# Experts' weights summed by group in one matmul per batch and spread over the partitions by loads from DRAM

## The reference

```python
x = x + tanh(g_xattn[1]) * xattn1(layernorm(x), ctx, mask)
x = x + tanh(g_ffn[1]) * moe(layernorm(x), ...)
# moe, for each token:
probs = softmax(x @ gate_weight.T)                 # 32 experts
top_val, top_idx = top_k(probs, 8); top_val /= sum(top_val)
w_tg = sum over the chosen of top_val, by merge_groups[top_idx]    # 8 groups
gate, up = split(x @ gate_up_proj[dominant_experts].T)   # 8 groups of 192 rows each
act = silu(gate) * up
out = sum over groups g of w_tg[:, g] * (act[:, g] @ down_proj[dominant_experts][g].T)
```

## Time and profile before

| | us |
|---|---|
| median of 3 runs | 1887.24 (1886.98 to 1889.6) |
| profiled execution | 1887.19 |
| span of the profiled execution | 1885.4 |
| TensorE busy in the span | 1846.4 (98%) |
| VectorE busy | 995.9 (53%) |
| ScalarE busy | 538.6 (29%) |
| GpSimd busy | 323.5 (17%) |

### The profile page before, as it was taken

The page is one execution under the profiler, slowest core; times in us unless marked ns, Lnnn a source line. Parts: engine busy times, 40 slices in busy tenths (PEclk is TensorE's granted clock), DMA queues, the critical chain, the costliest instruction groups (busy, mean ns, idle before and its releaser), DMA issues.

```text
span 1885.4 us, 24612 instructions
## 1 busy us (share of the span) xinstructions
PE 1846.4 (98%) x9552; PEld 905.6 (48%) x9552; DVE 995.9 (53%) x2036; ACT 538.6 (29%) x801; POOL 323.5 (17%) x299
## 2 busy tenths in 40 slices
PE   8799999999999999999999999999999999999999
PEld 3445554644444444444444444444444444444444
DVE  5676776754554455454436554545445455554422
ACT  3224433312221122122112233233333223333321
POOL 1123322222021120202010011111111111111111
PEclk9899999999999999999999999999999999999999
DMA  5124433333414223340310200101010101000000
GB/s 159 55 62 129 140 118 95 96 129 65 104 42 127 90 68 104 70 125 27 90 54 9 76 1 23 32 1 54 1 54 1 54 1 54 1 23 1 1 23 23
DMA packets 135830, 112.10 MB, mean 59 GB/s; under 512 B 75554, under 2 KB 92066, under 8 KB 135714
## 3 DMA queue, kind: packets, MB, share of 16 engines
q1 hardware_dynamic: 135714, 110.53, 19.7%
HBM read 78.00 MB, written 32.51 MB: 59 GB/s over the span
## 4 chain that ended last, share of the span: by engine, by line
PE 83%; issue 9%; DVE 3%; POOL 2%; DMA 2%; ACT 1%; POOLq 0%; SPq 0%; DVEq 0%; ACTq 0%
PE bank L923 44%; PE bank L1012 17%; PE bank L1092 10%; PE bank L992 4%; PE bank L932 3%; PE bank L977 1%; POOL arena L897 1%; PE bank L958 1%; PE bank L1079 1%; PE bank L1027 1%; POOL arena L871 0%; PE bank L1054 0%; DVE arena L1278 0%; DMA arena<-in_L_xattn_Wkv 0%; DMA arena<-x_after_ffn 0%
## 5 line engine op out<-in xcount | busy, mean ns | idle before, releaser
L923 PE MATMUL bank<-arena 128*128 128x512 f16 x4608 | 1042.2, 380 | 8.4 <-DVE arena L1299 7.3
L923 PEld LDWEIGHTS bank<-arena 128*128 128x128 f16 x4608 | 451.1, 98 | 538.9 <-DVE arena L1299 7.8
L1012 PE MATMUL bank<-arena 128*128 128x512 f16 x1536 | 352.1, 379 | 1.2 <-DVE arena L1506 1.2
L1092 PE MATMUL bank<-arena 128*128 128x512 f16 x1152 | 264.3, 379 | 0.9 <-POOL arena L897 0.9
L1648 DVE SCALAR_TENSOR_TENSOR arena<-bank,arena 128x512 f32<-128x512 f32 x96 | 72.0, 750 | 329.0 <-PE bank L923 329.0
L1191 ACT ACTIVATE arena<-bank,arena 128x512 f32<-128x512 f32 x128 | 99.5, 778 | 493.5 <-PE bank L923 490.5
L1012 PEld LDWEIGHTS bank<-arena 128*128 128x128 f16 x1536 | 150.1, 98 | 181.1 <-DVE arena L1506 1.7
L897 POOL TENSOR_TENSOR arena<-arena 128x512 f16<-128x512 f32 x96 | 111.0, 1157 | 626.0 <-ACT arena L1228 626.0
L1504 DVE TENSOR_SCALAR arena<-arena 128x512 f16<-128x512 f32 x128 | 65.8, 514 | 281.6 <-ACT arena L1191 281.3
L1092 PEld LDWEIGHTS bank<-arena 128*128 128x128 f16 x1152 | 112.0, 98 | 128.4 <-POOL arena L897 1.4
L1506 DVE SCALAR_TENSOR_TENSOR arena<-arena 128x512 f16<-128x512 f32 x128 | 118.0, 922 | 4.6
(11 more groups left out here) (159 smaller groups left out, 1215.8 us busy)
## 6 DMA issues: line engine op xcount, KB each, us to landing
arena<-in_L_ffn_proj SPq DMA_DIRECT2D x64, 256.0 KB, 2.9
arena<-in_L_ffn_gate_up_proj SPq DMA_DIRECT2D x96, 96.0 KB, 2.0
x_after_attention<-arena SPq DMA_DIRECT2D x8, 1024.0 KB, 5.2
arena<-x_after_attention SPq DMA_DIRECT2D x8, 1024.0 KB, 5.6
x_after_ffn<-arena SPq DMA_DIRECT2D x8, 1024.0 KB, 4.3
arena<-x_after_ffn SPq DMA_DIRECT2D x8, 1024.0 KB, 6.2
arena<-in_x SPq DMA_DIRECT2D x7, 1024.0 KB, 5.5
normalised_blocks<-arena SPq DMA_DIRECT2D x28, 256.0 KB, 2.0
```

The source lines that it names most:

```text
L923: m = e.matmul(bank[b][:, :], wT[l][:, c, tile * P:(tile + 1) * P], y[h][:, c, :], start=n == 0, stop=n == NPASS - 1)
L1012: m = e.matmul(bank[t][:, :], hv[h][:, 0, t * P:(t + 1) * P], w2T[l][:, j, :], start=j == 0 and i == 0, stop=j == NH - 1 and i == 2)
L1092: m = e.matmul(bank[t][:, :], hv[h][:, 0, t * P:(t + 1) * P], dnT[l][:, j, :], start=j == 0 and i == 0, stop=j == NR - 1 and i == 2)
```

## The change

Instead of one matmul per group and batch, `gsum` makes one per batch, right after `rturn`: it sums the experts' weights by group, so that 8 partitions hold the 8 groups. ScalarE scales them into `gsum_s`, SP stores them to a small tensor in DRAM, and for each group SP loads one row of 512 values back, repeated over all 128 partitions, into `gw_s` (`gload`, 256 KB, 64 times). VectorE's `mix` waits for that load. The side work of stage E is taken in three portions per step, the additional one between `ge` and `ue`; its pauses are set anew. In stage F the list `block_tasks` has 12 portions (before: 17).

```diff
+        return ([lambda: stats((0, 1)), lambda: stats((2, 3))] + [lambda t=t: tile(t) for t in range(NT)]
+                + [None] * 3 + [lambda: whole((0, 1)), lambda: whole((2, 3)), None])
...
-        return ([stats] + [lambda t=t: step(t) for t in range(NT + 1)] + [lambda: add("bload", i)]
-                + [None] * 6 + [lambda c=c: whole(c) for c in range(NC)])
...
-        return [L[0], both(split, L[1]), L[2], L[3], L[4], L[5], L[6],
-                lambda: add("scores", b, banks=1), lambda: None, lambda: add("pturn", b, banks=1),
-                lambda: add("read", b, banks=NT), *M, lambda: add("router", b, banks=1), lambda: None, lambda: None,
-                lambda: add("rturn", b, banks=1)]
+        pause = [None] * (1 if b == 0 else 2)
+        return [L[0], both(split, L[1]), *L[2:], lambda: add("scores", b, banks=1), *pause,
+                lambda: add("pturn", b, banks=1), lambda: add("read", b, banks=NT), *M,
+                lambda: add("router", b, banks=1), *pause, *pause, lambda: add("rturn", b, banks=1), *pause, lambda: add("gsum", b, banks=1)]
...
+    def apart():
+        f = side.pop(0) if side else None
+        if f:
+            f()
...
             add("ge", b, j, banks=1)
+            apart()
             add("ue", b, j, banks=1)
-            if side:
-                side.pop(0)()
+            apart()
             for gg in range(j * P // INTER, ((j + 1) * P - 1) // INTER + 1):
                 if gg * INTER >= j * P:
-                    add("bw", b, gg, banks=1)
+                    add("gload", b, gg)
             add("mix", b, j)
...
+            elif kind == "gsum":
+                b = step[1]
+                w.wait_ge(gs_ok, nth[step])
+                e.dma_start(gscr[b], gsum_s[0:NG, :]).then_inc(gs_out, 16)
+            elif kind == "gload":
+                _, b, gg = step
+                m = nth[step]
+                w.wait_ge(gs_out, 16 * (b + 1))
+                if m <= 3:
+                    w.wait_ge(down_mm, DN2 * NB)
+                else:
+                    w.wait_ge(mixed, mix_last(m - 3))
+                e.dma_start(gw_s[(m - 1) % 3], gscr[b, gg].partition_broadcast(P)).then_inc(gw_in[(m - 1) % 3], 16)
...
-                e.matmul(bank[k][:, :], onehot[:, gg * P:(gg + 1) * P], wTs[b % 2], start=True, stop=True).then_inc(bw_mm)
+                e.matmul(bank[k][:, :], of_group, wTs[b % 2], start=True, stop=True).then_inc(gs_mm)
...
-                e.activation(gw_s[(n - 1) % 3], bank[bank_of[step, 0]][:, :], ACT.Copy, scale=sc["kd"]).then_inc(bw_ok)
+                e.activation(gsum_s[0:NG, :], bank[bank_of[step, 0]][0:NG, :], ACT.Copy,
+                             scale=sc["kd"][0:NG, :]).then_inc(gs_ok)
...
-                    w.wait_ge(bw_ok, NG * b + gg + 1)
-                    of = gw_s[(NG * b + gg) % 3]
+                    of, k = gw_s[(NG * b + gg) % 3], NG * b + gg
+                    w.wait_ge(gw_in[k % 3], 16 * (k // 3 + 1))
                     e.tensor_tensor(r[rows, :], of[rows, :], m[rows, :], ALU.mult).then_inc(mixed)
```

More of the change, by code:

```diff
@@ L156, in weights_until, with block_tasks, stats, tile @@
             flush()
+    def block_tasks(i):
+        def stats(ts):
+            for t in ts:
+                add("stat", i, t)
+            if NT - 1 in ts:
+                add("rs", i)
+        def tile(t):
+            add("norm", i, t)
+            add("block", i, t)
+            add("bstore", i, t)
+            if t == NT - 1:
+                add("bload", i)
+        def whole(cs):
+            for c in cs:
+                add("whole", i, c)
+        return ([lambda: stats((0, 1)), lambda: stats((2, 3))] + [lambda t=t: tile(t) for t in range(NT)]
+                + [None] * 3 + [lambda: whole((0, 1)), lambda: whole((2, 3)), None])
     def ln_tasks(i, apart=False):
@@ L408, in make_plan @@
     while side:
-        side.pop(0)()
+        f = side.pop(0)
+        if f:
+            f()
     add("xload", "E", 1)
     add("xload", "E", 2)
+    def apart():
+        f = side.pop(0) if side else None
+        if f:
+            f()
     total = NB * NR
@@ L436, in make_plan @@
             side = attention_tasks(b + 1)
-        if side:
-            side.pop(0)()
+        apart()
     return P_
 def build(nc, x_in, ctx_in, ctx_t, mask_in, gx_in, gf_in, wq, wg, bg, wkv, wo, w1, b1, w2, b2,
-          gw, gup, dnp, mg, dom, xa, xb, yscr, out, stack):
+          gw, gup, dnp, mg, dom, xa, xb, yscr, gscr, out, stack):
     plan = make_plan()
@@ L512, in build @@
     wcat = small(NT * P // 2, F16).rearrange("p (t s) -> p t s", t=NT)
-    onehot = small(NG * P // 2, F16)
+    of_group = small(P // 2, F16)
+    gsum_s = small(TOK)
     ctr = small(NC * CTX).rearrange("p (c s) -> p c s", c=NC)
@@ L594, in build @@
     r_mm, rout, r_exp, r_turned, r_copied = (sem(n) for n in ("r_mm", "rout", "r_exp", "r_turned", "r_copied"))
-    ge_mm, silu, ue_mm, prod, bw_mm, bw_ok, mixed, m_hi, m_lo, dn_mm = (
-        sem(n) for n in ("ge_mm", "silu", "ue_mm", "prod", "bw_mm", "bw_ok", "mixed", "m_hi", "m_lo", "dn_mm"))
+    ge_mm, silu, ue_mm, prod, gs_mm, gs_ok, mixed, m_hi, m_lo, dn_mm = (
+        sem(n) for n in ("ge_mm", "silu", "ue_mm", "prod", "gs_mm", "gs_ok", "mixed", "m_hi", "m_lo", "dn_mm"))
+    gs_out, gw_in = sem("gs_out"), [sem(f"gw_in{i}") for i in range(3)]
     SOFT, ROUT = 13, 21
@@ L646, in freed @@
             return prod, n
-        assert kind == "bw"
-        return bw_ok, n
+        assert kind == "gsum"
+        return gs_ok, n
     x_slot = {("A", b): b % 3 for b in range(NB)}
@@ L821, in pool_program @@
         e.memset(bmask, 0.0).then_inc(const)
-        e.memset(onehot, 0.0).then_inc(const)
+        e.memset(of_group, 0.0).then_inc(const)
         e.memset(wcat[:, :, :], 0.0).then_inc(const)
@@ L1073, in tensor_program @@
                 project(step, upT, j, yT[b % 2], ue_mm)
-            elif kind == "bw":
-                _, b, gg = step
+            elif kind == "gsum":
+                b = step[1]
                 k = bank_free(step)
-                w.wait_ge(r_copied, b + 1)
+                w.wait_ge(r_copied, n)
                 w.wait_ge(dconst, 13)
-                e.matmul(bank[k][:, :], onehot[:, gg * P:(gg + 1) * P], wTs[b % 2], start=True, stop=True).then_inc(bw_mm)
+                e.matmul(bank[k][:, :], of_group, wTs[b % 2], start=True, stop=True).then_inc(gs_mm)
             elif kind == "dn":
@@ L1216, in scalar_program @@
                              scale=inv["gate"]).then_inc(silu)
-            elif kind == "bw":
-                _, b, gg = step
-                w.wait_ge(bw_mm, n)
+            elif kind == "gsum":
+                w.wait_ge(gs_mm, n)
                 w.wait_ge(cd_ok, 1)
-                if n > 3:
-                    w.wait_ge(mixed, mix_last(n - 3))
-                e.activation(gw_s[(n - 1) % 3], bank[bank_of[step, 0]][:, :], ACT.Copy, scale=sc["kd"]).then_inc(bw_ok)
+                if n > 1:
+                    w.wait_ge(gs_out, 16 * (n - 1))
+                e.activation(gsum_s[0:NG, :], bank[bank_of[step, 0]][0:NG, :], ACT.Copy,
+                             scale=sc["kd"][0:NG, :]).then_inc(gs_ok)
             elif kind == "mix":
@@ L1409, in vector_program @@
                 for gg in range(NG):
-                    e.tensor_scalar(onehot[0:2 * NE, gg * P:(gg + 1) * P], ones[0:2 * NE, :], mgf[0:2 * NE, :],
-                                    float(gg), ALU.mult, ALU.is_equal).then_inc(dconst)
+                    e.tensor_scalar(of_group[0:2 * NE, gg:gg + 1], mgf[0:2 * NE, :], float(gg), None,
+                                    ALU.is_equal).then_inc(dconst)
             elif kind == "ctxmax":
@@ L1637, in vector_program @@
                 if b > 1:
-                    w.wait_ge(bw_mm, NG * (b - 1))
+                    w.wait_ge(gs_mm, b - 1)
                 e.tensor_copy(wTs[b % 2], bank[bank_of[step, 0]][:, :].bitcast(F16)[:, 0:TOK]).then_inc(r_copied)
@@ L1704 @@
     yscr = nc.dram_tensor("normalised_blocks", (2, TOK, D), F32, kind="Internal").ap()
+    gscr = nc.dram_tensor("group_weights", (NB, NG, TOK), F32, kind="Internal").ap()
     out = nc.dram_tensor("out", (NB, TOK, D), F32, kind="ExternalOutput").ap()
     with ExitStack() as stack:
-        build(nc, *args, xa, xb, yscr, out, stack)
+        build(nc, *args, xa, xb, yscr, gscr, out, stack)
     r = run_bass_kernel_spmd(nc, [arrays], core_ids=[0])
```

## The result

The changed kernel takes **1917.96 us** (1916.57 to 1920.83) against 1887.25 us of the kernel before: ratio 1.0161, with a 95% interval of [1.0148, 1.0174] (ratios further down are given in the same way). It is slower by 31 us. The forecast was 1895: the sign and the place were right, the size was wrong, and the time lies above the stated range.

The account below looks back on a forecast made before the run. TensorE was taken to set the time in stages E and F. 1887.2 - 12.3 (matmuls) + 12.0 (batch stalls) + 4.8 (start of E) + 3.4 (clock) = 1895.1 us; own range 1890 to 1903, 8 in 10 within 1877 to 1905.

Parts of the forecast that it names:

- the sign: Whole kernel: the change makes it slower, by 0.4%, with a chance of 0.58 for slower.
- The gain: Stage E: 56 fewer matmuls on TensorE at 0.22 us each save 12.3 us.
- The place of the stalls: Stage E: TensorE stalls 4.8 us at its start and 12.0 us over batches 1 to 5; none in 6 and 7.
- The landing: Stage E: `gload(b, 1)` lands 0.7 us after the last context load, bounds 0 and 1.4 us.
- The chain from the landing to `dn`, 2.6 us: Stage E: from the load's landing, `mix` and GpSimd's rest take 2.6 us until the operand of `dn` is ready.
- The clock, 3.4 us: Stage E: slower TensorE clock after the two longest stalls costs 2 x 1.7 us; bounds nothing and 10.2.
- rival 3: Stage E: the clock falls after each stall and a `gload` costs 1.4 us, giving 1906 us; chance 0.10.
- Stage F at nothing: Stage F: the 12 portions may make ScalarE wait some 3 us, but cost TensorE nothing; bound 0 to 3 us.

Follow-up runs that it names:

- experiment 9: Changed kernel with `gload(b, 1)` ahead of store and load, stage F's old 17 portions, three empty portions before batch 0's side work: 1874.61 us.
- Experiment 1: Changed kernel with `gload(b, 1)` issued together with `gload(b, 0)`, ahead of the batch's store and load: 1884.76 us.
- experiments 7 and 8: Changed kernel with `xload` of batches 3 to 7 issued behind `gload(b, 1)`: 1905.85 us; with it five steps later still: 1895.35 us.
- experiments 2 to 4: Changed kernel with stage F's old list: 1910.93 us; kernel before with the new list: 1894.45 us, and with its bias three portions later: 1888.12 us.

## Why the prediction was wrong

- **The gain** of 12.3 us: right (12.2 by the batches' length, 13.7 +- 3 by experiment 9).
- **The place of the stalls**: right, six of them, with `gload(b, 1)` behind store, `xload` and context loads, and none in batches 6 and 7. Experiment 1 shows the cause.
- **The landing**: right. "0.7 us behind the last context load" was 0.63 in batch 2. At the start of stage E the stall of 4.8 us came out as forecast. That these loads wait for what is in front of them holds; that only what is in front counts does not (experiments 7 and 8).
- **The chain from the landing to `dn`, 2.6 us, taken as the path that ends last: the first step that failed.** The chain itself holds: in batch 2 GpSimd's rest ends 2.6 us after the landing. But another path ends later. The chain was read from a trace in which one group of transposes stands before that `dn`. Now three do; the prediction counted the other two with their length and not with what they wait for. The third needs a norm that stands on VectorE behind the first transposes' halves, whose copy on ScalarE waits behind the rounding of `mix`. The path from the landing to the transposes takes 3.1 us and the transposes at half clock 0.9: 4.0. The prediction named what is queued on VectorE behind `mix`, but neither followed it back to TensorE nor looked at ScalarE's queue. So TensorE's idle time was 23.3 us in the six places where 16.8 were summed. This is read from the trace; no run tested it alone.
- **The clock, 3.4 us: the second step that failed, and the larger one.** It was charged for the two long stalls, because rows of 1.20 and 4.04 us were nearest to either side. It fell after all six, after 3.3 us as well. Losses in stage E are 38.5 us and idle time 23.3; the other 15.2 us, 1.9 to 3.1 per stall, 2.5 on average, come almost wholly from work at 1.2 GHz (waits without a fall of the clock cost 0.2 us beyond themselves in experiments 7 and 8). That is more than the upper bound of 10.2. Part of this error comes from the first: measured, all six stalls (3.3 to 5.1 us) lie nearer to the row of 4.04, and by the prediction's own reading all six would have been charged. The rest is the price, 2.5 instead of 1.7. That the clock falls each time was rival 3, with a chance of 0.10. The Trainium skill (TensorE: Matmul & The Clock Gate, "HAM oscillation") says that a wait for a DMA between groups of matmuls can put the engine back to the half rate, and that this is then paid at each such wait: the trace agrees for these six, and experiments 7 and 8 have shorter waits after which the clock stayed.
- **Stage F at nothing: the third.** It was bounded by 3 us for ScalarE's waits in `whole`. These came (seven, of at most 3.4 us) and, as forecast, did not reach TensorE. It lost 5.3 us another way: the shorter list moves the weights' work in time, so that VectorE's part of it runs beside GpSimd's additions and in another order (experiments 2 to 4). The prediction had not followed the turns that the list leaves over.

Sum of the corrections: 23.3 - 16.8 = 6.5 of idle time, 15.2 - 3.4 = 11.8 of clock (6.8 for the four stalls that were not charged, 5.0 for the price), 5.3 of stage F, 23.6 us in all; 1895 + 23.6 = 1919.

## What to carry to other kernels

When a value that an engine made is to come by DMA instead, write down what stands in front of each such load in its issue queue, waits included, and what is large around it in flight; the load that comes once per batch behind a store and a reload decides, not the median one. On a TensorE that is busy throughout, a stall of 3.3 us or more cost about 2.5 us more than its idle time here, as slower matmuls behind it, and stalls of up to 2.7 us cost 0.2 more (experiments 7 and 8): count both. Follow a late value to TensorE on every queue behind it, not only along its own chain. A list of side work that is shortened moves everything that fills its gaps: look at what the moved pieces will meet.

## What the runs showed that was not expected

- A load of 256 KB took 5.7 to 6.0 us with 1 MB issued before it, 4.0 to 5.7 with 1 MB issued right after it, and 3.6 to 4.6 with neither. The Trainium skill's rule that descriptors are consumed in ring order (DMA: Bandwidth & Descriptors, "Queues, rings and completion order") agrees with the first; here the second shows that what comes later in the same queue can slow a load too.
- After 3.36 us without a matmul the granted clock was 0.50, after 84 matmuls of zeros in the waits it was 1.00: matmuls with zero weights keep the clock, and paid 9.4 us net.
- VectorE's `tensor_scalar` of 128x512 took 1.48 us beside GpSimd's additions and 0.48 without.
